# Row stage and router stage of a graph network, written as one stage in five parts

## The reference

```python
x = x + gnn0(layernorm(x))            # ends in relu(batchnorm(h @ W2 + b2))
t = layernorm(x)
logits = t @ Wr + br                  # Wr: 256 x 8; top 2 of 8 experts a token
x = x + experts(t, logits)
g = gnn1(layernorm(x))                # ends in relu(batchnorm(h) + layernorm(x))
x = x + g
t = layernorm(x)
gates = softmax(t @ gW + gb)          # gW: 256 x 4; top 2 of 4
x = x + mlp(t, gates)
```

## Time and profile before

| what | us |
|---|---|
| median of 3 runs | 5695.61 |
| lowest, highest | 5695.45, 5719.21 |
| the profiled execution | 5692.53 |
| its span | 5690.8 |
| TensorE busy | 3907.4 (69%) |
| GpSimd busy | 3004.5 (53%) |
| VectorE busy | 2066.0 (36%) |
| ScalarE busy | 1935.9 (34%) |
| TensorE's mean granted clock | 0.832 of 2.4 GHz |

### The profile page before, as it was taken

One profiled execution on the slowest core, in us unless ns is written; L12 is line 12 of the kernel. 1 busy time (PEld: TensorE's weight loads), 2 busy tenths in 40 slices (PEclk: granted clock), 3 DMA queues, 4 the chain that ended last, 5 costly groups with the idle time before them and its releaser, 6 DMA issues. The chain is left out here.

```text
span 5690.8 us, 77820 instructions
## 1 busy us (share of the span) xinstructions
PE 3907.4 (69%) x16120; PEld 3044.7 (54%) x16121; DVE 2066.0 (36%) x5417; ACT 1935.9 (34%) x4772; POOL 3004.5 (53%) x2633
## 2 busy tenths in 40 slices
PE   2666666666577599999765565667555556664798
PEld 2555555555475488888544444446344445453665
DVE  5444444455456511111422222234422222336333
ACT  2222222223243222222243333333633333336422
POOL 2888888888800022222047777774277777760000
PEclk9777788888886799999777878888777787886699
DMA  6666666666640355555323333331233333320000
GB/s 225 88 88 88 88 89 88 88 88 88 82 145 0 132 181 191 177 192 177 124 89 101 102 102 102 101 101 50 85 101 101 102 101 102 102 79 0 15 22 19
DMA packets 353879, 568.89 MB, mean 100 GB/s; under 512 B 61598, under 2 KB 274460, under 8 KB 350993
## 3 DMA queue, kind: packets, MB, share of 16 engines
q0 software_dynamic: 198720, 337.81, 29.4%
q1 hardware_dynamic: 150820, 226.00, 12.1%
q10 hardware_dynamic: 4268, 4.30, 0.2%
HBM read 404.84 MB, written 163.07 MB: 100 GB/s over the span
## 5 line engine op out<-in xcount | busy, mean ns | idle before, releaser
L638 POOL DMA_INDIRECT T<-h_rows,segment_sum_idx x1568 | 1546.0, 986 | 727.3 <-issue 395.0
L674 PE MATMUL bank<-T 128*128 128x256 f32 x3904 | 1239.2, 481 | 811.8 <-PEq L69 811.1
L674 PEld LDWEIGHTS bank<-T 128*128 128x128 f32 x3904 | 916.3, 244 | 1134.1 <-issue 974.1
L392 POOL DMA_INDIRECT node_sums<-T,scattered_sum_idx x784 | 1214.3, 1549 | 343.8 <-issue 218.2
L654 ACT ACTIVATE T<-T,segment_sum_edge 128x256 f32<-128x256 f32 x1568 | 667.9, 496 | 1180.0 <-DMA T<-h_rows,segment_sum_idx 1180.0
L463 PE MATMUL bank<-X,T 128*128 x1952 | 631.9, 481 | 103.5 <-PEq L69 100.3
L457 PE MATMUL bank<-T 128*128 128x128 f32 x1952 | 342.2, 331 | 418.5 <-PEq L69 418.3
L701 DVE TENSOR_TENSOR A<-A,bank 128x256 f32 x488 | 205.2, 421 | 1110.0 <-DVEq L69 1109.8
L463 PEld LDWEIGHTS bank<-X,T 128*128 128x128 f32 x1952 | 462.8, 249 | 203.3 <-issue 125.9
L457 PEld LDWEIGHTS bank<-T 128*128 128x128 f32 x1952 | 300.7, 233 | 431.0 <-issue 426.6
L498 DVE SCALAR_TENSOR_TENSOR T<-T,edges,not_after 128x128 f32<-128x128 int16 x784 | 223.8, 348 | 543.9 <-DVEq L69 499.4
(11 more groups left out here) (285 smaller groups left out, 4759.2 us busy)
## 6 DMA issues: line engine op xcount, KB each, us to landing
T<-in_L_ffn_W SPq DMA_DIRECT2D x52, 1024.0 KB
A<-in_L_ffn_W SPq DMA_DIRECT2D x52, 1024.0 KB, 8.6
T<-src_lanes SPq DMA_DIRECT2D x196, 128.0 KB, 3.2
T<-h_rows,segment_sum_idx POOLq DMA_INDIRECT x1568, 2.7
node_sums<-A SPq DMA_DIRECT2D x3, 6528.0 KB, 33.5
A<-node_sums SPq DMA_DIRECT2D x36, 512.0 KB, 5.2
h_rows<-A SPq DMA_DIRECT2D x50, 256.0 KB, 2.1
node_sums<-T,scattered_sum_idx POOLq DMA_INDIRECT x784, 3.8
```

Of the source, the lines that this page charges most:

```text
L392: pool.indirect_dma_start(c.sum_dram[at % COPIES], bass.IndirectOffsetOnAxis(ap=idx[:, h % LR, j:j + 1], axis=0), msg[:, h % LR * G + j, : ...
L638: pool.indirect_dma_start(msg[:, h * G + j, :], None, c.h_dram, bass.IndirectOffsetOnAxis(ap=idx[:, h, j:j + 1], axis=0)).then_inc(landed[ ...
L674: mm = pe.matmul(acc[s][:, 0:D], hot[:, s, j, :], msg[:, h * G + j, :], start=(j == 0), stop=(j == G - 1))
```

## The change

The row stage and the router stage become one stage at both places. The 25 blocks are put in five parts, of 3, 5, 5, 6 and 6 blocks. A list written out by hand gives the order of work for all engines: the rows of a part, its sums, the first two blocks of the next part, the roots of the part, then its blocks turned one by one, with a block of the next part's rows behind each turn while there are any. The loops are written out.

- Row stage: as before, per block, in "rows" items.
- Statistics: `finish_stats` is split in `begin_stats` (seven VectorE instructions) and `finish_roots`, on a part's tiles.
- Normalising for the router: on GpSimd (two `tensor_scalar` of 128x256 a block) instead of ScalarE.
- Out of PSUM: ScalarE copies the turned block, into `back[s]` or straight into `c.T`, instead of VectorE.
- Logits: the router weights are the stationary operand (128x8 or 128x4), the block's 256 columns the moving one; the result is 8 or 4 partitions by 256. ScalarE copies it to SBUF (`lists`), TensorE turns it back in two small transposes, all blocks into one bank, and VectorE adds the bias once at the end.

Cut to its core:

```diff
-def norm_to_rows(nc, c, residual):
...
+ROW_PARTS = ((0, 6), (6, 16), (16, 26), (26, 38), (38, 50))
+def rows_in_parts():
+    blocks_of = [list(range(lo // 2, hi // 2)) for lo, hi in ROW_PARTS] + [[]]
+    order = [("rows", j) for j in blocks_of[0]] + [("sums", 0)]
+    for n in range(len(ROW_PARTS)):
+        here, later = blocks_of[n], blocks_of[n + 1]
+        order += [("rows", j) for j in later[:2]] + [("root", n)]
+        later = later[2:]
+        for u in range(max(len(here), len(later))):
+            order += [("turn", j) for j in here[u:u + 1]] + [("rows", j) for j in later[u:u + 1]]
+        if n + 1 < len(ROW_PARTS):
+            order.append(("sums", n + 1))
+    return order
...
         @block.gpsimd
+            for n, j in enumerate(turns):
+                s = n % 2
+                pool.wait_ge(normed_to, part_of_block(j) + 1)
+                if n >= 2:
+                    take(pool, row_free[s])
+                for q in range(2):
+                    t = j * 2 + q
+                    ins = pool.tensor_scalar(row[s][:, q, :], c.X[:, t, :], c.rstd[:, t:t + 1], c.shift[:, t:t + 1], ALU.mult, ALU.add)
+                ins.then_inc(row_ready[s], 1)
         @block.scalar
+            def cols_of(j):
+                s = j % 2
+                if j >= 2:
+                    take(act, cols_free[s])
+                if not moe:
+                    if j >= 2:
+                        take(act, sum_free[s])
+                    norm_block(act, c, sum_[s], j).then_inc(residual_ready[s], 1)
+                apply_affine(act, c, col[s], cols_block(c, j), ACT.Relu if moe else ACT.Identity).then_inc(cols_ready[s], 1)
+            def keep_list(n):
+                s = n % 2
+                take(act, lg_ready[s])
+                if n >= 2:
+                    take(act, list_free[s])
+                act.copy(lists[s], lg[s][0:ne, 0:BLK]).then_inc(list_ready[s], 1)
+            def turn(n, j):
+                s = n % 2
+                take(act, turned[s])
+                act.sem_inc(row_free[s], 1)
+                act.copy(in_cols(j), turn2[s][:].rearrange("p (k n) -> p k n", k=KD)).then_inc(back_ready[s], 1)
+                if n >= 1:
+                    keep_list(n - 1)
+            for kind, j in order:
...
+            keep_list(NJ - 1)
             if moe:
                 root(act, go, done, scale2)
-            if moe:
-                blocks(act, norm)
-            else:
-                two_ahead(act, norm, to_t)
         @block.tensor
+            def turn_cols(j):
+                s = j % 2
+                take(pe, cols_ready[s])
+                if j >= 2:
+                    take(pe, rows_free[s])
                 for q in range(2):
                     for k in range(KD):
+                        mm = pe.transpose(turn[s][:, q * D + k * P:q * D + (k + 1) * P], col[s][:, k, q * P:(q + 1) * P], c.ident[:])
+                mm.then_inc(rows_turned[s], 1)
+            def logits_of(n):
+                s = n % 2
+                take(pe, back_ready[s])
+                for k in range(KD):
+                    mm = pe.matmul(lg[s][0:ne, 0:BLK], wr[:, k, :], in_cols(turns[n])[:, k, :], start=(k == 0), stop=(k == KD - 1))
+                mm.then_inc(lg_ready[s], 1)
+            def lists_back(n):
+                s, j = n % 2, turns[n]
+                take(pe, list_ready[s])
+                for q in range(2):
+                    t = j * 2 + q
+                    mm = pe.transpose(logits[:, t * ne:(t + 1) * ne], lists[s][:, q * P:(q + 1) * P], c.ident[0:ne, 0:ne])
+                mm.then_inc(logits_done if n == NJ - 1 else list_free[s], 1)
+            def turn_rows(n):
+                s = n % 2
+                take(pe, row_ready[s])
+                if n >= 1:
+                    logits_of(n - 1)
+                turn_to_cols(pe, c, row[s], turn2[s]).then_inc(turned[s], 1)
+                if n >= 2:
+                    lists_back(n - 2)
             pe.wait_ge(w_in, 32)
-            ahead(pe, turn_rows, logits)
+            for kind, j in order:
...
+            logits_of(NJ - 1)
+            lists_back(NJ - 2)
+            lists_back(NJ - 1)
         @block.vector
-            finish_stats(dve, go, done, c, v)
+            dve.wait_ge(w_in, 32)
+            for kind, j in order:
+                if kind == "rows":
+                    add(j)
+                elif kind == "sums":
+                    dve.drain().then_inc(v, 1)
+                    take(dve, v)
+                    begin_stats(dve, go, c, v, slice(*ROW_PARTS[j]))
+                elif kind == "root":
+                    finish_roots(dve, done, c, v, slice(*ROW_PARTS[j]))
+                    dve.sem_inc(normed_to, 1)
...
-            ahead(dve, copy, read)
+            take(dve, logits_done)
+            chain(dve, tt(logit, logits[:, 0:n3].rearrange("p (t e) -> p t e", e=ne), br[:][:, None, :].to_broadcast([P, NB, ne]), ALU.add), v)
```

More of the change, by code:

```diff
@@ L1273, in router @@
     XC = 10
+    order = rows_in_parts()
+    turns = [j for kind, j in order if kind == "turn"]
     def run(block, sb, sem):
         wr, br = sb("wr", [P, KD, ne]), sb("br", [P, ne])
-        row = [sb(f"row{s}", [P, 2, D]) for s in range(2)]
         col = [sb(f"col{s}", [P, KD, BLK]) for s in range(2)]
+        sum_ = None if moe else [sb(f"sum{s}", [P, 2, D]) for s in range(2)]
+        lists = [carve(flat(c.A), 8400 + s * BLK, (BLK,))[0:ne] for s in range(2)]
+        row = [carve(flat(c.A), 9000 + s * 2 * D, (2, D)) for s in range(2)]
+        back = [carve(flat(c.A), 10100 + s * KD * BLK, (KD, BLK)) for s in range(2)]
         work = flat(c.T) if moe else flat(c.A)[:, NB * D // 2:]
         n3 = NB * ne
-        logit, prob, eid, cand, pick1, pick2 = (carve(work, i * n3, (NB, ne)) for i in range(6))
+        logit, prob, cand, pick1, pick2 = (carve(work, i * n3, (NB, ne)) for i in range(5))
+        eid = sb("eid", [P, NB, ne])[:]
         small = [carve(work, 6 * n3 + i * NB, (NB,)) for i in range(12)]
@@ L1351, in _ @@
+            n = 0
+            for kind, j in order:
+                if kind == "rows":
+                    cols_of(j)
+                elif kind == "root":
+                    lo, hi = ROW_PARTS[j]
+                    root(act, go, done, c.rstd[:, lo:hi])
+                elif kind == "turn":
+                    turn(n, j)
+                    n += 1
+            keep_list(NJ - 1)
             if moe:
                 root(act, go, done, scale2)
[L1353 to L1357, removed]
@@ L1408, in _ @@
                         n = q * HB + u
[L1409 removed]
+                        mm = pe.matmul(c.ps[7][:, 0:COLS], hot_slot[r][:, u, :], hot_tile[r][:, u, :],
                                        start=(n == 0), stop=(n == n2 - 1))
@@ L1568, in _ @@
                 take(dve, listed[r])
-            chain(dve, dve.scalar_tensor_tensor(full[:], c.ps[6][:, 0:COLS], 0.25, slots[:], ALU.add, ALU.add), v)
+            chain(dve, dve.scalar_tensor_tensor(full[:], c.ps[7][:, 0:COLS], 0.25, slots[:], ALU.add, ALU.add), v)
             dve.tensor_copy(c.out_idx[:], full[:]).then_inc(v, 1)
```

91 lines of the change are left out of this document (46 added, 45 removed).

## The result

The changed kernel takes 5804.91 us, median of 4 runs (5797.32 to 5810.34), against 5698.35 for the kernel before in the same session (4 runs, 5695.45 to 5719.21): 1.0178 times as long, 95% interval 1.0156 to 1.0199. It is slower. The forecast of 5826.5 is 22 us too high, and the result lies in the range.

What follows compares the result with a forecast made beforehand. No engine was full over the span; the two rewritten places, 265.9 us, were on the path. Place 1 +63 and place 2 +71 gave +134 on 5692.5: 5826.5 us, own range 5775 to 5860, range with the clock rival 5725 to 5860.

Steps and rivals of the forecast that it cites:

- A pair costs the sum, not the larger: Turn followed by a row block: ScalarE and TensorE work add up, 6.4 us in place 1, 7.5 in place 2.
- A turn alone 4.0: Turn with no row block behind it: 4.0 us against 2.56 before, 7 intervals per place.
- Boundaries 17.3, 13.0 twice, 6.8: Intervals between parts in place 1, in us: first 17.3, two of 13.0, last, without rows, 6.8.
- Heads 20.2 and 23.8, tails 5.9 and 4.9: Start and end of places 1 and 2, in us; heads include waiting for small weight loads.
- the five row blocks: In place 1's head: VectorE's first five row blocks, 9.85 us at 1.97 each.
- the second square root: In place 1's tail: it now comes last and adds another 1 us.
- GpSimd 0.55 an operation: GpSimd's tensor_scalar: 0.55 us taken, between 0.31 and 0.58, counting only where a part starts.
- What was costed at nothing: Semaphore instructions, SP's load list, GpSimd's iotas: no cost; written-out code could separately lose 0 to 5 us.
- Rival (a): TensorE's clock rises in both places: 84 us off the forecast, 5743 us, still slower; chance 0.23.
- Rival (b): Pairs overlap, busiest engine sets the pace: faster at high clock, -11 us at low; chances 0.09 and 0.03.
- the fast form of (b): Overlapping pairs with high clock: both places 189 us against 266, -77, 5616 us; chance 0.09.
- Rival (c): GpSimd binds if an operation takes over 2 us or 3.2 per pair: 5857 to 5950 us; chance 0.03.

Runs made afterwards that it cites:

- e1: Changed kernel, but ScalarE copies each logits list two more times into scratch; both places 385.1 us, whole kernel 5814.42 us.
- e3: Changed kernel, but the logits product takes only the first half of the features; both places 337.9 us, whole kernel 5775.66 us.
- e5: Changed kernel, but TensorE turns the next block before the column transposes of the row block; both places 279.0 us, whole kernel 5715.05 us.
- e6: Changed kernel, but the logits product and its list copy come one turn late; both places 269.9 us, whole kernel 5688.26 us.
- e2: Changed kernel, but GpSimd normalises each block twice, first into scratch; both places 381.3 us, whole kernel 5804.84 us.
- e4: Changed kernel with one part of 25 blocks, all rows before all turns; both places 274.3 us, whole kernel 5706.96 us.
- e12: Changed kernel with four scrap 128-column TensorE products behind every turn; 5760.26 us, 1.0117 times the kernel before.
- e11: Changed kernel with two parts (12 and 13 blocks), turn before rows on TensorE, logits product one turn late; 5639.69 us, 0.9901 times the kernel before.
- e7: Changed kernel with turn before rows on TensorE and logits product one turn late; both places 249.5 us, whole kernel 5676.23 us, one run.
- e9: The e7 kernel unchanged, measured again with 12 runs; 5681.23 us, 0.9973 times the kernel before.

## Why the prediction was right, point by point

- **A pair costs the sum, not the larger.** Right, and shown by e1, e3, e5 and e6. Forecast 6.4 and 7.5; at the low clock 6.26 and 7.23. The timeline of the pair above gives the steps: 0.75 from copy to affine (forecast 0.99), 1.38 to the column transposes (1.34), 1.01 to the logits (0.85), 1.81 to the turn (1.86), 1.31 to the next copy (1.34). In place 1, 13 such intervals, as counted.
- **A turn alone 4.0.** 3.83 at the low clock, 2.54 at the high one. 7 of them, as counted.
- **Boundaries 17.3, 13.0 twice, 6.8.** 16.7, 11.97, 12.0 and 6.5 in place 1. In place 2 20.0, 14.7, 14.9 and 5.5, for 20.6, 15.6, 15.6 and 6.8.
- **Heads 20.2 and 23.8, tails 5.9 and 4.9.** 19.2 and 23.6, 4.2 and 3.8. The head of place 1 can be read step by step:

```profile
1756.68 0.91 DVE L1471 SCALAR_TENSOR_TENSOR X<-X,mean,bank 128x256 f32<-128x256 f32 x2 [5.34 <-DVEq L69]
...
1758.49 0.85 DVE L1471 SCALAR_TENSOR_TENSOR X<-X,mean,bank 128x256 f32<-128x256 f32 x2
...
1760.25 0.86 DVE L1471 SCALAR_TENSOR_TENSOR X<-X,mean,bank 128x256 f32<-128x256 f32 x2
...
1768.89 2.17 POOL L1342 TENSOR_SCALAR A<-X,rstd,shift 128x256 f32<-128x256 f32 x4 [15.32 <-DVEq L1496]
```

VectorE starts 4.5 us in, as forecast (2.7 and 1.8). The term that was too large is the five row blocks: 9.2 us for 9.85, as a block takes 1.76 us here and not 1.97. Another 0.3 lies in the sums, the turn and its hand-over. The tails can't be compared as they stand, since that of place 1 ran at a clock of 1.00 and that of place 2 at 0.50. At equal clock place 1's is 1.2 to 1.3 us longer (5.02 in e2 and 3.78 at 0.50; 4.18 and 2.86 in e5 at 1.00), near the 1 us that the second square root was costed at.
- **GpSimd 0.55 an operation.** 0.554. It lay near the upper bound of the earlier trace rows, as its kind does. The best case in the Trainium skill's GPSIMD Engine Reference, Performance versus the Vector engine, gave an estimate of 0.77 for two; the trace has 1.1.
- **What was costed at nothing.** With the head's steps accounted for as above, none is left for semaphore instructions. For code written out, 0 to 5 us of loss were allowed; it gained. In the loop of before, VectorE's row blocks start alternately 1.87 and 2.06 us apart, written out 1.76. Place 2 shows no such gain: 2.78 a block before and 2.81 in e4.
- **Smaller slips.** The "5.5 us" of a block of place 2 in the kernel before is 2.67 + 2.56 = 5.2 by the prediction's own rows, 5.3 with VectorE's mean of 2.78. The sum does not use it.

**The term that was mis-sized is the clock.** The sum took 0.50 throughout, "pair 6.4" and "turn alone 4.0" for every one. The trace has .62 and .59: of 13 pairs in place 1, three are at 6.26, one at 6.0 for want of a list, seven between 5.7 and 6.0 at clocks of 0.55 to 0.74, two at 4.5, and three of the seven lone turns are at 2.54. Forecast and measurement differ by 33.4 us over both places (400.2 and 366.8). By the intervals, 15.3 of it is mostly the clock: in place 1 the 13 pairs take 74.7 where 13 x 6.26 are 81.4, and three lone turns save 1.29 each; in place 2 the pairs take 91.9 where 13 x 7.23 are 94.0, and two lone turns save 1.3 each. In that, 0.5 is not the clock but the list that the first turn of each place does not have. Another 7.7 is the pairs' and turns' own size (0.14 and 0.27 a pair, 0.17 a turn), 6.4 the boundaries, 4.0 heads and tails: 33.4. The boundaries and tails have some clock in them too (0.65 in two boundaries of place 1), and the boundaries VectorE's shorter row blocks. The whole kernel's forecast is only 21.6 us too high, and that is luck: the unchanged stages took 3.9 us more in the profile of the changed kernel, and its median lies 7.6 above the profiled execution.

**Rival (a)**, the clock rises, was given 0.23 and came in part. Its price for the full case was right: a pair of 6.4 - 1.8 = 4.6 at the high clock, measured 4.50. The argument against it, that the old router loop was busy throughout at 0.50, did not carry over: the new stage is less busy by the records (92.8 us of 168.2) and had the higher clock. The Trainium skill's TensorE: Matmul & The Clock Gate, What's actually happening, has the activity of TensorE release the clock; e12 agrees with its direction (0.83 for 0.50 in the first pairs), the old router loop does not (0.50 with 62.1 of 64.0 us busy).

**Rival (b)**, the pairs overlap, was priced at 4.0 us a block at the low clock and at VectorE's 1.97 at the high one. The changed kernel does not do it: its pairs are at 4.50 even at the high clock. e11, where TensorE's queue has no gap, has pairs of 2.20, by TensorE, and takes 5639.69 us where the fast form of (b) had 5616. **Rival (c)** is out by the 0.554 us of an operation, and by e2.

## What to carry to other kernels

When two in-order queues feed each other in a fused loop, write the loop's round trip down as one list and add it up: if an item of the one queue waits for the item just issued on the other, idle engines don't help, and every operation added on either side counts whole. (Every run here had two copies of each tile, and the wait was there all the same; no run had more.) Issuing the consumer one turn late, and the item the other engine waits for first, made 2.2 us of 4.5 here, both at the high clock, without changing one operation. Then make the parts of a fused stage few and large: the interval across a boundary took 8 to 18 us with five parts and the queues reordered, two parts beat five by 38 us in the places, and thirteen, in an order of their own, lost most of what the reordering had won.

## What the runs showed that was not expected

- Work that nobody reads made the kernel faster. 100 products more on TensorE in place 1 raised its granted clock there from .62 to .82 and took 18.8 us off the place; in place 2 the same took 10.3 us off. Which property of the work raises the clock stays open: the old router loop, TensorE busy for 62.1 of 64.0 us by the records, stayed at 0.50. The scrap was plain products; no run added transposes in their place.
- The clock in the places goes with the code, down to edits that leave TensorE's work alone. With GpSimd's work doubled, place 1 had .57 against .62 and was 12.8 us longer, of which the head and boundaries explain about 5. The same kernel profiled on two chips (e7 and e9) had the same intervals within 0.02 us and the same clock in both places.
- A small copy out of a bank (8x256, 0.36 us alone) costs 0.26 us when another follows it on ScalarE.
